# Reciprocal deviations by a power on GpSimd in place of a root on ScalarE and its refinement on VectorE

## The reference, cut to what matters

```python
def _layernorm(x, axis=-1, eps=1e-05):
    m = jnp.mean(x, axis=axis, keepdims=True)
    v = jnp.var(x, axis=axis, keepdims=True)
    return (x - m) / jnp.sqrt(v + eps)
...
xn = xf * jax.lax.rsqrt(jnp.mean(xf * xf, axis=-1, keepdims=True) + eps)
logits = xn @ router_w.T
...
xn = _layernorm(x, axis=-1)
x = x + _L0_attn_ref(xn, L0_attn_U) + _L0_ffn_ref(xn, ...)
```

## Time and profile before

| | us |
|---|---|
| median of 3 runs | 158.22 |
| lowest and highest | 157.16 and 158.99 |
| span of the profiled execution, first to last instruction | 156.0 |
| median less span | 2.2 |
| TensorE busy in that span | 151.1 (97%) |
| VectorE, ScalarE, GpSimd busy | 117.5, 103.8, 83.3 |

### The profile page before, as it was taken

How to read it: one execution, slowest core, us unless ns; L and a number is a source line. 1 busy time by engine, 2 the same in 40 slices (tenths; PEclk the granted TensorE clock), 3 DMA queues, 4 the chain that set the end, 5 groups by cost and what they waited for, 6 DMA issues and landing times.

```text
span 156.0 us, 3115 instructions
## 1 busy us (share of the span) xinstructions
PE 151.1 (97%) x964; PEld 135.6 (87%) x964; DVE 117.5 (75%) x290; ACT 103.8 (67%) x217; POOL 83.3 (53%) x102
## 2 busy tenths in 40 slices
PE   6899999999999999999999999999999999999992
PEld 6878878798999988888878999999999999878992
DVE  3799969899824599999997676786787786545962
ACT  3258999999479398768756669899686566343200
POOL 7562531357777778878400004698988857454000
PEclk9999999999999999999999999999999999999999
DMA  4999999992111117536059400314232111118477
GB/s 118 278 274 119 147 277 335 345 335 77 57 53 51 51 32 220 158 80 191 0 119 299 136 0 2 149 39 119 60 105 70 32 46 34 29 29 263 100 267 217
DMA packets 26640, 20.72 MB, mean 133 GB/s; under 512 B 2334, under 2 KB 22841, under 8 KB 26625
## 3 DMA queue, kind: packets, MB, share of 16 engines
q1 hardware_dynamic: 24832, 17.89, 44.3%
q0 software_dynamic: 1792, 2.65, 5.6%
HBM read 12.36 MB, written 7.92 MB: 130 GB/s over the span
## 4 chain that ended last, share of the span: by engine, by line
PE 92%; DMA 2%; ACT 2%; DVE 2%; POOL 1%; issue 1%; SPq 0%
PE bank L1257 9%; PE bank L1342 9%; PE bank L1177 8%; PE bank L1179 8%; PE bank L1178 8%; PE bank L1282 8%; PE bank L1288 8%; PE bank L1285 8%; PE bank L1398 5%; PE bank L1400 5%; PE bank L1399 5%; PE bank L1414 2%; PE bank L1242 2%; DMA acc<-in_L_attn_x_dram 2%; PE bank L1425 2%; PE bank L1197 1%
## 5 line engine op out<-in xcount | busy, mean ns | idle before, releaser
L676 ACT ACTIVATE silu<-bank 128x512 f32<-128x512 f32 (+1 forms) x64 | 33.3, 520 | 29.3 <-PE bank L1288 29.1
L570 POOL DMA_INDIRECT slots_dram<-row,slot_i x32 | 34.0, 1063 | 10.9 <-issue 9.4
L1008 DVE TENSOR_TENSOR bank<-bank,silu 128x320 f32<-128x320 f32 (+1 forms) x48 | 27.1, 565 | 15.6 <-ACT silu L676 12.6
L589 POOL DMA_INDIRECT routed_dram<-eo,xg x24 | 23.0, 957 | 11.5 <-DVE eo L1048 6.3
L1014 DVE TENSOR_TENSOR hid_lo<-bank,hid_hi 128x320 fp32r<-128x320 f32 (+1 forms) x48 | 26.2, 546 | 0.0
L684 ACT CAST hid_hi<-bank 128x320 fp32r<-128x320 f32 (+1 forms) x48 | 22.9, 477 | 0.0
L577 POOL TENSOR_TENSOR ew_lo<-sw_raw,ew_hi 128x1024 fp32r<-128x1024 f32 x3 | 7.2, 2416 | 19.4 <-ACT ew_hi L700 19.4
L1342 PEld LDWEIGHTS bank<-sd,hid_s 128*128 128x128 f32 x128 | 14.8, 192 | 0.3
L1008 DVE TENSOR_TENSOR hid_s<-bank,silu 128x512 f32<-128x512 f32 x16 | 11.0, 685 | 5.5 <-PE bank L1179 5.2
L1257 PEld LDWEIGHTS bank<-row,probs 128*128 128x128 f32 x128 | 14.8, 192 | 0.2
L1342 PE MATMUL bank<-sd,hid_s 128*128 128x128 f32 x128 | 15.0, 275 | 0.0
(11 more groups left out here) (204 smaller groups left out, 363.8 us busy)
## 6 DMA issues: line engine op xcount, KB each, us to landing
sw_raw<-in_L_ffn_rg_dram SPq DMA_DIRECT2D x8, 256.0 KB, 3.0
sw_raw<-in_L_ffn_ru_dram SPq DMA_DIRECT2D x8, 256.0 KB, 3.5
rd_raw<-in_L_ffn_rd_dram SPq DMA_DIRECT2D x8, 256.0 KB, 3.4
routed_dram<-fill SPq DMA_DIRECT2D x1, 2048.0 KB, 12.6
routed<-routed_dram SPq DMA_DIRECT2D x8, 256.0 KB, 4.0
slots_dram<-fill SPq DMA_DIRECT2D x1, 1300.0 KB, 12.6
xg<-slots_dram SPq DMA_DIRECT2D x8, 130.0 KB, 2.4
row<-row SPq DMA_DIRECT2D x1, 1024.0 KB, 8.2
```

The costliest lines, as they stand in the source:

```text
L570: G.indirect_dma_start(slots_dram, bass.IndirectOffsetOnAxis(slot_i[:, k, t:t + 1], 0), row[:, t, 0:RW], None, bounds_check=E * CAP - 1, o ...
L676: C.activation(silu[:, q % 2, 0:n], gate_bank(q)[:, 0:n], ACT.Silu).then_inc(silu_ready, 1)
L1008: V.tensor_tensor(hid, up[:, 0:n], silu[:, q % 2, 0:n], ALU.mult).then_inc(hid_ready, 1)
```

## The change

GpSimd sets a tile `minus_half` (128x32) to -0.5, behind `seg` and before the padding of `xg`, and waits for it. It then raises `ve` to that power in each pass, one instruction a pass (128x8 and 128x24): ahead of its own `normalize(0)`, and behind `split_shared(1)` and ahead of U's lower part. ScalarE's two roots go, with the wait that led them, and so do VectorE's four instructions in each pass; VectorE waits for GpSimd's `rstd` and goes on with the shift.

```diff
-        root = sb("root", [P, 2, NT])
-        nw_a = sb("nw_a", [P, 2, NT])
-        nw_b = sb("nw_b", [P, 2, NT])
-        nw_c = sb("nw_c", [P, 2, NT])
+        minus_half = sb("minus_half", [P, 2, NT])
...
             pool.wait_ge(consts, 1)
+            G.memset(minus_half[:, :, :], -0.5).then_inc(power_set, 1)
+            pool.wait_ge(power_set, 1)
             G.memset(xg[TAIL:P, :, 2, :], 0.0).then_inc(xg_padded, 1)
...
+            def rstd_of(gs):
+                ts = slice(TG * gs[0], TG * (gs[-1] + 1))
+                pool.wait_ge(ve_ready, pass_of[gs[0]] + 1)
+                G.tensor_tensor(rstd[:, :, ts], ve[:, :, ts], minus_half[:, :, ts], ALU.pow).then_inc(rstd_ready, 1)
+
+            rstd_of(PASSES[0])
             normalize(0)
             split_shared(0)
             split_shared(1)
+            rstd_of(PASSES[1])
             pool.wait_ge(U_hi_s, 1)
-            pool.wait_ge(rstd_ready, len(PASSES))
...
-            def root_of(gs):
-                ts = slice(TG * gs[0], TG * (gs[-1] + 1))
-                act.wait_ge(ve_ready, pass_of[gs[0]] + 1)
-                C.activation(root[:, :, ts], ve[:, :, ts], ACT.Sqrt, scale=0.25).then_inc(root_ready, 1)
...
-            root_of(PASSES[0])
             normalize(0)
...
             round_shared(2)
-            root_of(PASSES[1])
             silu_chunk(0)
...
-            def rstd_of(gs):
+            def shifts_of(gs):
 
                 ts = slice(TG * gs[0], TG * (gs[-1] + 1))
-                n = pass_of[gs[0]] + 1
-                dve.wait_ge(root_ready, n)
-                then(V.reciprocal(nw_a[:, :, ts], root[:, :, ts]))
-                then(V.tensor_tensor(nw_b[:, :, ts], nw_a[:, :, ts], ve[:, :, ts], ALU.mult))
-                then(V.scalar_tensor_tensor(out=nw_c[:, :, ts], in0=nw_b[:, :, ts], scalar=0.25,
-                                            in1=root[:, :, ts], op0=ALU.mult, op1=ALU.add))
-                V.reciprocal(rstd[:, :, ts], nw_c[:, :, ts]).then_inc(rstd_ready, 1)
-                dve.wait_ge(rstd_ready, n)
+                dve.wait_ge(rstd_ready, pass_of[gs[0]] + 1)
                 V.scalar_tensor_tensor(out=nmr[:, ts], in0=mv[:, ts, 0], scalar=-1.0, in1=rstd[:, 0, ts],
                                        op0=ALU.mult, op1=ALU.mult).then_inc(nmr_ready, 1)
```

More of the change, by code:

```diff
@@ L314, in moe_attention_kernel @@
         ve_ready = sem("ve_ready")
-        root_ready = sem("root_ready")
+        power_set = sem("power_set")
         rstd_ready, nmr_ready = sem("rstd_ready"), sem("nmr_ready")
@@ L1066, in _ @@
             variances_of(PASSES[0])
-            rstd_of(PASSES[0])
+            shifts_of(PASSES[0])
             normalize(0)
@@ L1074, in _ @@
             split_router()
-            rstd_of(PASSES[1])
+            shifts_of(PASSES[1])
             normalize(1)
```

## The result

The changed kernel takes 161.62 us (median; 161.12 to 162.27) against 157.69 of the kernel before: a ratio of 1.0258, with a 95% interval of 1.022 to 1.0296. It is 3.9 us slower, where 158.1 and no change that could be told had been forecast. The profiled execution has a span of 160.3 us. The first rival came true: the power is dear, and pass 1 decides most of the loss.

The account below looks back on a forecast made before the run. TensorE, holding 92% of the chain that ended last, was taken to bound the kernel. Pass 0 giving -0.39 and pass 1 costing 0.29 made -0.10 us, so 158.22 became 158.1 us, range 157.2 to 162.0.

Parts of the forecast that it names:

- The first rival: Pass 1: power dear, VectorE idles on GpSimd and its queue delays `project(3)`; 4.1 us slower at 80 steps; chance 0.33.
- the price of the power: GpSimd, both passes: 25 steps of 2.4 ns, so 0.06 us an element, plus a fixed 0.17 us.
- d8: Time of GpSimd's power of 128x8 in pass 0, taken as 0.65 us.
- d24: Time of GpSimd's power of 128x24 in pass 1, taken as 1.61 us.
- the end nearer the rows: Choice of 25 steps for the power, from an estimate of 20 to 50, or 80 if exact to the last bit.
- estimate from 4 cycles for a dependent step: Power on GpSimd at 3.3 ns a step and 25 steps: d8 0.83, d24 2.16, together +0.6 us.
- The path and the sum: Pass 0 moves TensorE by the larger of -0.40 and d8 - 1.04, pass 1 by the larger of 0 and d24 - 1.32.
- The floor: Pass 0: TensorE's 60 small matmuls end at 7.38, ahead of the first transposes, so at most 0.40 us is gained.
- GpSimd is free by then: Pass 0: GpSimd's constants and added memset end at 5.41, before the power can begin at 5.63.
- One table load less by 14 us: ScalarE should show one table load less by 14 us; the 1.28 us load was costed at nothing.
- The clock: Sign: TensorE's clock falling below 1.00 would mean something outside the account; no size given.
- The stall of pass 1: TensorE's wait for `xnT_lo` near 20 us should be 0.2 to 0.6 us; over 1 us means the first rival.

Follow-up runs that it names:

- the product: The changed kernel with the power replaced by a product of the same two tiles, the constant 1 in place of -0.5: 157.16 against 157.41, ratio 0.9972.
- the run of pass 0 alone: The kernel before with the power on GpSimd in pass 0 only, ScalarE's root there still run but unused: 158.13, ratio 1.0048.
- the run of pass 1 alone: The kernel before with the power on GpSimd in pass 1 only: 160.16, ratio 1.0178.

## Why the prediction was wrong

- **The term that was mis-sized is the price of the power.** The prediction had a step cost 2.4 ns and took 25 steps, 0.06 us an element: d8 = 0.65 and d24 = 1.61. Measured are 1.68 and 4.20: 0.158 us an element, 66 such steps, and a fixed part of 0.42 instead of 0.17. The choice of the end nearer the rows was the mistake: a sum of the same form says nothing about the function inside it. The fixed part alone shows that, since it too is more than twice the sum's. The prediction's estimate from 4 cycles for a dependent step (the Trainium skill: GPSIMD Engine Reference, Performance pitfalls for Q7 kernels) pointed the right way, with 0.6 us, and was still too low at 25 steps; no run here shows such a chain by itself.
- **The path and the sum held.** The formulas gave d8 - 1.04 for pass 0 and d24 - 1.32 for pass 1. With the measured 1.68 and 4.20 they give 0.64 and 2.88, together 3.52 us; measured were 0.72 and 2.75 alone. Together it was 3.52 in the set where the clock seldom fell (160.96 against 157.44), to the second digit by luck: the other two sets, with two launches each at 0.989, gave 3.9 and 4.1.
- **The range** reached to 162.0, so 161.62 lies in it, but only because it was drawn out to 77 steps; its likeliest part ended at 159.8. The base was high too: 158.22 was the median of three launches, four have 157.69, and the later ones 157.3 to 157.4. And where time and span of one launch are both on record, the span is 1.7 to 1.8 us shorter, not 2.2.
- **The first rival** had its mechanism and nearly its price right: 4.1 us at 80 steps, 3.5 at the measured price, plus 1.0 in launches where the clock fell.
- **The floor** of pass 0 was right in kind: the product gained at most some 0.25 us, not clear of the noise, of the 0.8 that the chain lost. But 7.38 isn't fixed. The small matmuls ended between 6.1 and 7.4 us in these profiles, and the weights' transfer holds TensorE right behind them.
- **"GpSimd is free by then" failed.** It held for the one profile, in which x came at 4.33. Where x came earlier, the power stood behind the zeroing until 5.3 us, as in the run of pass 0 alone. The added memset is on the path there; the cover was a matter of the launch. In that run the transposes of sequence 0 start at 8.12, in the run of pass 1 alone, which keeps the root there, at 7.15: 0.97 us apart, not 0.64. So the near agreement of 0.72 with 0.64 is luck in part (its interval goes from 0.4 to 1.1).
- **The table load stays.** "One table load less by 14 us" was wrong: ScalarE loads a table for its first function at 0.78 and silu's at 12.20. It was costed at nothing, and the product's run shows no cost.
- **The clock** was named only as a sign of something outside the account, and that it was: this stall had a second price, in 7 of 24 launches.
- **Where TensorE waits.** The stall of pass 1 was looked for at 20 us, ahead of `project(3)`. It shows first at the transposes of sequence 1 (1.76 us), since the excess was far above that place's slack. The end is still set at `project(3)` when the clock holds.

## What to carry to other kernels

An operation that no row shows has no price from its neighbours of the same form: when its bounds lie on both sides of the decision, measure it alone on an idle engine before moving it onto the path. Ask of a slow operation what part of its result is due first: in that order the same powers cost nothing. And count a stall of TensorE twice, once for its length and once for what the clock may take behind it (here about 1.0 us, in some launches).

## What the runs showed of the hardware

A power on GpSimd costs 0.42 us and 0.158 us for each element of a row, so 1.68 us for 128x8, against 0.197 us for a product of 128x8. The three exponents tried differ by 5%, and 16 partitions cost no less than 128.

VectorE's small writes of `ve` stretch while GpSimd zeroes a tile. In the profile of the changed kernel they ended just as the zeroing of `lgT` (4.81 + 0.53) did, by VectorE's timeline:

```profile
4.97 0.40 DVE L864 TENSOR_SCALAR ve<-mv 128x4 f32<-128x4 f32 x1
5.05 0.33 DVE L865 TENSOR_SCALAR ve<-mv 128x4 f32<-128x4 f32 x1
```

With the zeroing moved away (in the changed kernel) they took 0.17 and 0.16:

```profile
4.58 0.17 DVE L865 TENSOR_SCALAR ve<-mv 128x4 f32<-128x4 f32 x1
4.66 0.16 DVE L866 TENSOR_SCALAR ve<-mv 128x4 f32<-128x4 f32 x1
```

The Trainium skill (GPSIMD Engine Reference, Specifications) says that the two engines share their way into the on-chip memory and contend in some forms of VectorE's instructions; the rows agree, and put it at 0.23 us for the first write here. In the eight profiles in which such a write was stretched, it ended within 0.04 us of the zeroing that it overlapped, so it took what was left of that: 0.21 to 0.55 us for the first of the two.
